# One probability tile in four transposed by a DMA instead of TensorE, and value projections in units of 512 pixels

## The reference

```python
def _L0_conv_ref(x, W_theta, b_theta, W_phi, b_phi, W_fuse, b_fuse):
    t, p, g = conv1x1(x, W_theta), conv1x1(x, W_phi), x          # 64, 64 and 128 channels
    f = softmax(einsum('ndq,ndk->nqk', t, p) / sqrt(64))
    return x + conv1x1(einsum('nqk,nck->ncq', f, g), W_fuse, b_fuse)

def _L1_conv_ref(x, gn_w, gn_b, q_w, ..., p_b):
    h_ = group_norm(x, gn_w, gn_b)                               # 32 groups
    q, k, v = conv1x1(h_, q_w, q_b), conv1x1(h_, k_w, k_b), conv1x1(h_, v_w, v_b)
    attn = softmax(einsum('bic,bcj->bij', q, k) * 128 ** -0.5)
    return x + conv1x1(einsum('bcj,bij->bci', v, attn), p_w, p_b)
```

## Time and profile before

| | before |
|---|---|
| time of three runs, median (lowest to highest) | 2015.87 us (2015.73 to 2016.52) |
| the profiled execution | 2016.01 us |
| its span | 2014.1 us |
| PE busy | 1975.8 us, 98% |
| DVE busy | 1727.1 us, 86% |
| ACT busy | 1546.7 us, 77% |
| POOL busy | 1356.0 us, 67% |
| mean granted TensorE clock | 0.994 |
| DMA | 68.01 MB |

### The profile page before, as it was taken

The page is one execution under the profiler, slowest core; times in us unless marked ns, Lnnn a source line. Parts: engine busy times, 40 slices in busy tenths (PEclk is TensorE's granted clock), DMA queues, the critical chain, the costliest instruction groups (busy, mean ns, idle before and its releaser), DMA issues.

```text
span 2014.1 us, 40574 instructions
## 1 busy us (share of the span) xinstructions
PE 1975.8 (98%) x11526; PEld 1334.6 (66%) x11526; DVE 1727.1 (86%) x2976; ACT 1546.7 (77%) x2696; POOL 1356.0 (67%) x1766
## 2 busy tenths in 40 slices
PE   6899999999999999999999999999999999999998
PEld 4666666666666666666666666666666666666664
DVE  6788888888888888888888888888888888888885
ACT  5677777777777777777777777777777778877775
POOL 4667666766667776667676677766676767777664
PEclk8999999999999999999999999999999999999999
DMA  1101111011111011110111110111101111101100
GB/s 53 48 27 37 36 34 37 23 36 42 36 31 36 26 36 36 42 31 21 41 37 36 31 36 26 36 36 42 31 23 40 36 36 31 36 26 37 33 6 22
DMA packets 29117, 68.01 MB, mean 34 GB/s; under 512 B 3616, under 2 KB 4512, under 8 KB 29088
## 3 DMA queue, kind: packets, MB, share of 16 engines
q1 hardware_dynamic: 29088, 67.65, 11.2%
HBM read 34.08 MB, written 16.78 MB: 25 GB/s over the span
## 4 chain that ended last, share of the span: by engine, by line
PE 76%; DVE 14%; issue 6%; ACT 3%; DVEq 0%; POOL 0%; DMA 0%; SPq 0%; ACTq 0%; POOLq 0%
PE o_ps L370 27%; PE s_ps L370 20%; PE t_ps L384 18%; DVE neg_raw L701 5%; PE m_ps L370 5%; PE m_ps L491 4%; DVE et L686 3%; ACT e L612 2%; DVE phi L769 1%; PE m_ps L493 1%; DVE x L720 1%; DVE theta L756 1%; DVE rden L677 1%; ACT et L548 0%; PE m_ps L475 0%
## 5 line engine op out<-in xcount | busy, mean ns | idle before, releaser
L863 POOL TENSOR_SCALAR e<-e,rden 128x1024 f32<-128x1024 f32 x512 | 575.8, 1125 | 482.3 <-DVE rden L677 479.2
L548 ACT ACTIVATE et<-t_ps 128x512 f16<-128x512 f32 x1024 | 560.3, 597 | 387.6 <-PE t_ps L384 387.2
L686 DVE TENSOR_TENSOR et<-t_ps,et 128x512 f16<-128x512 f32 x1024 | 659.7, 683 | 126.9 <-ACT et L548 120.7
L370 PE MATMUL o_ps<-et,v_hi 128*128 128x512 f16 x2048 | 696.3, 381 | 2.4 <-DVE y_sb L728 2.1
L384 PEld LDWEIGHTS t_ps<-ident_sb,e 128*128 128x128 f32 x4096 | 476.1, 141 | 118.7 <-DVE et L686 17.1
L384 PE MATMUL t_ps<-ident_sb,e 128*128 128x128 f32 x4096 | 540.4, 274 | 5.4 <-POOL e L863 2.6
L370 PE MATMUL o_ps<-et,v_lo 128*128 128x512 f16 x1024 | 388.0, 379 | 0.0
L370 PEld LDWEIGHTS o_ps<-et,v_hi 128*128 128x128 f16 x2048 | 204.5, 100 | 236.9 <-issue 50.3
L612 ACT ACTIVATE e<-s_ps,neg_max,exp_scale 128x1024 f32<-128x1024 f32 x256 | 309.8, 1210 | 4.4 <-DVE neg_max L704 2.4
L701 DVE TENSOR_REDUCE neg_raw<-s_ps 128x1 f32<-128x1024 f32 x256 | 309.5, 1209 | 1.4 <-PE s_ps L370 1.4
L698 DVE TENSOR_REDUCE neg_max<-s_ps 128x1 f32<-128x1024 f32 x256 | 310.6, 1213 | 0.0
(11 more groups left out here) (129 smaller groups left out, 2316.9 us busy)
## 6 DMA issues: line engine op xcount, KB each, us to landing
xs<-in_x SPq DMA_DIRECT2D x32, 512.0 KB, 3.7
phi<-phi SPq DMA_DIRECT2D x64, 256.0 KB, 3.1
xr<-in_x SPq DMA_DIRECT2D x32, 512.0 KB, 3.3
out_y<-y_sb SPq DMA_DIRECT2D x64, 256.0 KB, 2.1
w_f<-in_w_fuse_t SPq DMA_DIRECT2D x1, 64.0 KB, 2.7
ident_sb<-in_ident SPq DMA_DIRECT2D x1, 64.0 KB, 2.2
p_t<-in_p_w_t SPq DMA_DIRECT2D x1, 64.0 KB, 2.1
v_n<-in_v_w SPq DMA_DIRECT2D x1, 64.0 KB, 2.3
```

The costliest lines, as they stand in the source:

```text
L370: mm = pe.matmul(out, lhs_t, rhs, start=start and n == 0, stop=stop and n == len(terms) - 1)
L548: nc.scalar.activation(et[t // GROUP % 2][:, t % GROUP, GROUP * half:GROUP * (half + 1), :], t_ps[half][:, :].rearrange("k (b q) -> k b q" ...
L686: nc.vector.tensor_tensor(tile[:, KB + GROUP * half:KB + GROUP * (half + 1), :], t_ps[half][:, :].rearrange("k (b q) -> k b q", b=GROUP), ...
L863: return nc.gpsimd.tensor_scalar(*args)
```

## The change

**One tile in four is crossed.** Tiles 0, 4, 8 and 12 (`t % 4 == 0`) are no longer normalised by POOL, transposed by PE and copied out by ACT and DVE. Instead DVE makes `rden_e`, a scaled reciprocal (slot t + 2); ACT writes `e * rden_e` in float16 as the high half of `pair` (slot t + 2, between the exponential and `take_unit`); DVE writes what is left as its low half (slot t + 3, where `take_lo` stood); and SP issues one transposing DMA of the pair, 512 KB, straight into `et` (slot t + 3). The group's value product waits for it.

**Value units** cover 512 pixels: four blocks, each of three products of 128 columns (high with high weights, low with high, high with low) that add up in PSUM. The bank leaves through `stage` as the sum, POOL's addition goes, and high and low parts are split over 512 columns at once. There are four such units an image instead of eight, and slots 3, 12, 13 and 15 have no unit; `stage` has two buffers instead of four.

```diff
 NORM_MAX = 64.0
-UNITS = {0: "gn1", 1: "gn2", 2: "v2", 3: "v3", 4: "k0", 5: "k1", 6: "q0", 7: "w0", 8: "q1",
-         9: "tp0", 10: "w1", 11: "tp1", 12: "w2", 13: "w3", 14: "v0", 15: "v1"}
-STAGES = 4
-STAGE = {name: n % STAGES for n, name in enumerate(UNITS[s] for s in range(SLOTS) if UNITS[s][0] in "vw")}
+CROSSED = (0,)
+UNITS = {0: "gn1", 1: "gn2", 2: "v1", 4: "k0", 5: "k1", 6: "q0", 7: "w0", 8: "q1", 9: "tp0", 10: "w1", 11: "tp1",
+         14: "v0"}
+STAGES = 2
+STAGE = {"v1": 0, "w0": 1, "w1": 0, "v0": 1}
 H_SLOT = 2
...
                 return t[b] if isinstance(b, int) else t[bass.ds(b, 1)].rearrange("a c n -> c (a n)")
+            def transposes(i, s):
+                t = s - T_LAG
+                if not here(crossed_at, i, t):
+                    return
+                r = CROSSED.index(t % GROUP)
+                sp.wait_ge(s_pair, before(crossed_at, i, t) + 1)
+                sp.sem_inc(s_carrier)
+                sp.wait_ge(s_pv, or_none(before(group_at, i, t - t % GROUP) - 1))
+                sp.sem_inc(s_carrier)
+                sp.dma_start_transpose(et[t // GROUP % 2][:, t % GROUP, :, :],
+                                       pair[:, r, :, :].rearrange("q a n -> q (a n)")).then_inc(s_pair_t[r], 16)
             def image_loads(i, s):
...
                 if quarter == 0:
-                    pe.wait_ge(s_tlo, 2 * before(tile_at, i, first + GROUP))
+                    pe.wait_ge(s_tlo, 2 * before(turned_at, i, first + GROUP))
+                    for r in range(len(CROSSED)):
+                        pe.wait_ge(s_pair_t[r], 16 * before(group_at, i, first) + 16)
                     if s == PV_LAG:
...
                     if name[0] in "vw":
-                        for b in range(2):
-                            px = slice((2 * part + b) * P, (2 * part + b + 1) * P)
-                            pe.matmul(out[:, 2 * b * C:2 * (b + 1) * C], hi[:, px],
-                                      w[:, :, :].rearrange("p a c -> p (a c)"), start=True, stop=False)
-                            mm = pe.matmul(out[:, 2 * b * C:(2 * b + 1) * C], lo[:, px], w[:, 0, :],
-                                           start=False, stop=True)
+                        for b in range(GROUP):
+                            px = slice((GROUP * half + b) * P, (GROUP * half + b + 1) * P)
+                            mm = product(out[:, b * C:(b + 1) * C], [(hi[:, px], w[:, 0, :]), (lo[:, px], w[:, 0, :]),
+                                                                     (hi[:, px], w[:, 1, :])])
                     else:
...
                 t = s - T_LAG
-                if not here(tile_at, i, t):
-                    return
-                if half == 0 and t % GROUP == 0:
-                    act.wait_ge(s_pv, or_none(before(group_at, i, t) - 1))
-                act.wait_ge(s_tr, 2 * before(tile_at, i, t) + 1 + half)
+                if not here(turned_at, i, t):
+                    return
+                if half == 0:
+                    act.wait_ge(s_pv, or_none(before(group_at, i, t - t % GROUP) - 1))
+                act.wait_ge(s_tr, 2 * before(turned_at, i, t) + 1 + half)
                 nc.scalar.activation(et[t // GROUP % 2][:, t % GROUP, GROUP * half:GROUP * (half + 1), :],
                                      t_ps[half][:, :].rearrange("k (b q) -> k b q", b=GROUP),
                                      ACT.Copy).then_inc(s_thi, 1)
+            def pair_hi(i, s):
+                t = s - 2
+                if not here(crossed_at, i, t):
+                    return
+                r = CROSSED.index(t % GROUP)
+                act.wait_ge(s_rden_e, before(crossed_at, i, t) + 1)
+                act.wait_ge(s_pair_t[r], 16 * before(group_at, i, t - t % GROUP))
+                nc.scalar.activation(pair[:, r, 0, :], e[:, t % 4, :], ACT.Identity,
+                                     scale=rden_e[:, t % 4:t % 4 + 1]).then_inc(s_pair_hi, 1)
             def take_unit(i, s):
...
                 act.wait_ge(s_max, n + 1)
-                act.wait_ge(s_tr, or_none(2 * n - 6))
+                if s % GROUP in CROSSED:
+                    act.wait_ge(s_pair, before(crossed_at, i, s - GROUP + 1))
+                else:
+                    act.wait_ge(s_tr, 2 * before(turned_at, i, s - GROUP + 1))
                 scale = exp_scale[:, 0:1] if s % SLOTS >= PHASE else 1.0
...
                     exponentials(i, s)
+                    pair_hi(i, s)
                     take_unit(i, s)
...
                 nc.vector.reciprocal(rden[:, c:c + 1], den[:, c:c + 1]).then_inc(s_rden, 1)
+                if here(crossed_at, i, s - 2):
+                    dve.wait_ge(s_rden, before(tile_at, i, s - 2) + 1)
+                    nc.vector.tensor_scalar(rden_e[:, c:c + 1], rden[:, c:c + 1], E_SCALE, None,
+                                            ALU.mult).then_inc(s_rden_e, 1)
             def take_lo(i, s, half):
                 t = s - T_LAG
-                if not here(tile_at, i, t):
-                    return
-                dve.wait_ge(s_thi, 2 * before(tile_at, i, t) + 1 + half)
+                if half == 0 and here(crossed_at, i, t):
+                    r = CROSSED.index(t % GROUP)
+                    dve.wait_ge(s_pair_hi, before(crossed_at, i, t) + 1)
+                    nc.vector.scalar_tensor_tensor(out=pair[:, r, 1, :], in0=e[:, t % 4, :],
+                                                   scalar=rden_e[:, t % 4:t % 4 + 1], in1=pair[:, r, 0, :],
+                                                   op0=ALU.mult, op1=ALU.subtract).then_inc(s_pair, 1)
+                if not here(turned_at, i, t):
+                    return
+                dve.wait_ge(s_thi, 2 * before(turned_at, i, t) + 1 + half)
                 tile = et[t // GROUP % 2][:, t % GROUP, :, :]
...
             def normalise(i, s):
-                if not here(tile_at, i, s - 2):
+                if not here(turned_at, i, s - 2):
                     return
...
                 name = UNITS[(s - 1) % SLOTS]
-                n = before(values_at, i, s - 1)
-                total, part = (stage[:, STAGE[name], :, t, :] for t in range(2))
+                n, half = before(values_at, i, s - 1), int(name[-1])
+                src = stage[:, STAGE[name], :]
                 pool.wait_ge(s_evac, before(unit_at, i, s - 1) + 1)
-                nc.gpsimd.tensor_tensor(total, total, part, ALU.add).then_inc(s_sum, 1)
                 pool.wait_ge(s_pv, before(group_at, i, 0) if name[0] == "w"
                              else before(group_at, i, PHASE if s > PHASE else -PHASE))
                 values = (v_hi[1], v_lo[1]) if name[0] == "w" else (v_hi[0], v_lo[0])
-                hi, lo = (v[:, 2 * int(name[-1]):2 * int(name[-1]) + 2, :] for v in values)
-                pool.wait_ge(s_sum, n + 1)
-                rounded(hi, total, s_split_hi)
+                hi, lo = (v[:, GROUP * half:GROUP * (half + 1), :].rearrange("p b c -> p (b c)") for v in values)
+                rounded(hi, src, s_split_hi)
                 pool.wait_ge(s_split_hi, n + 1)
-                rest(lo, total, hi, s_split)
+                rest(lo, src, hi, s_split)
             def body(i):
```

More of the change, by code:

```diff
@@ L98, in group_at, with crossed_at, turned_at @@
         return int(g % GROUP == GROUP - 1 and tile_at(g))
+    def crossed_at(g):
+        return int(tile_at(g) and g % GROUP in CROSSED)
+    def turned_at(g):
+        return int(tile_at(g) and g % GROUP not in CROSSED)
     def unit_at(g):
@@ L103, in unit_at @@
         name = UNITS.get(s)
-        if name in ("tp0", "tp1", "v0", "v1"):
+        if name in ("tp0", "tp1", "v0"):
             return int(-1 <= i <= NB - 2)
-        if name in ("v2", "v3"):
+        if name == "v1":
             return int(0 <= i < NB)
@@ L113, in direct_at @@
     def direct_at(g):
-        return int(UNITS[g % SLOTS][0] in "tqk" and unit_at(g))
+        return int(UNITS.get(g % SLOTS, "-")[0] in "tqk" and unit_at(g))
     def values_at(g):
-        return int(UNITS[g % SLOTS][0] in "vw" and unit_at(g))
+        return int(UNITS.get(g % SLOTS, "-")[0] in "vw" and unit_at(g))
     def gn1_at(g):
@@ L217, in attention_pair @@
         h_hi, h_lo = sb("h_hi", [C, N], F32R), sb("h_lo", [C, N], F32R)
-        stage = sb("stage", [P, STAGES, 2, 2, C])
+        stage = sb("stage", [P, STAGES, HALF])
         theta2 = sb("theta2", [C, N], F32R)
@@ L226, in attention_pair @@
         et = [sb(f"et{n}", [P, GROUP, 2 * KB, P], F16) for n in range(2)]
+        pair = sb("pair", [P, len(CROSSED), 2, N], F16)
+        rden_e = sb("rden_e", [P, 4])
         neg_raw = sb("neg_raw", [P, 4])
@@ L251, in bank @@
         def bank(i, s):
-            return o_ps if first_units(i) and UNITS[s] in ("tp1", "v1") else m_ps
+            return o_ps if first_units(i) and UNITS[s] == "tp1" else m_ps
         s_wload0 = sem("layer0_weights_loaded")
@@ L277, in attention_pair @@
         s_tlo = sem("et_lo_ready")
+        s_rden_e = sem("rden_e_ready")
```

(18 more changed lines are left out.)

## The result

The changed kernel takes 2030.34 us (median of four runs, 2028.76 to 2030.38) against 2015.80 us of the kernel before in the same session: 1.007 of it, 95% interval 1.0052 to 1.0087. It is slower by 14.5 us, 0.45 us for each of 32 images. The forecast was 2009 and faster; the sign is wrong.

A forecast was written before the change was run, and what follows sets the result against it. PE, busy 98%, was taken to bound the kernel, with DVE next at 86%. Savings and added waits summed to -0.22 us per image, -7 us over 32 images: forecast 2009 us, range 1984 to 2040.

The forecast's parts named there:

- Transposes gone: On PE, four of sixteen tiles need no transposes, 0.88 us each: -3.52 us per image.
- Value units: On PE, four units priced at 1.32 us replace eight old ones at 0.83 per two: +1.96 us per image.
- The slot 12 wait: PE's wait for the VectorE phi at slot 12 goes, as no unit is there now: -0.34 us per image.
- Slot 1: PE reaches slot 1's transposes 1.0 us early and waits for VectorE's low parts: +0.78 us per image.
- The +6.48: For slot 1, the first half of t_ps came free 6.48 us after x's start at slot 15.
- Slot 7: pair_hi ahead of q_hi on ACT delays q_lo, so unit w0 starts late: +0.5 us per image.
- Slots 3 and 13: Said to have slot 7's pattern with small remainders: +0.1 us each per image.
- VectorE and GpSimd: Pair subtraction may meet GpSimd's value rest on the shared port at slots 11 and 15: +0.2 us per image.
- rival 2: Shared port holds the pair subtraction at slots 11 and 15: 2023 us, 2037 if GpSimd is held too; chance 0.25.
- The break-even I named: Shared-port holds decide the outcome from 0.42 us per image on.
- The transfer: SP's transposing DMA has about 10 us to land before the next pair_hi; costed at nothing.
- rival 3: Transfer lands later than 10 us, so ACT waits at pair_hi four times an image; 11 us gives above 2050; chance 0.1.

The follow-up runs named there:

- no cross: Changed kernel with the new value units only and no tile crossed (CROSSED empty): 2059.4 us, ratio 1.0218 to the kernel before.
- the small rest: Changed kernel with GpSimd making the values' low part for 16 of 512 columns in the loop's images: 2015.9 us, ratio 1.0003 to the kernel before.
- old units: Changed kernel keeping the crossing but restoring eight value units of 256 pixels and the GpSimd addition: 2047.0 us, ratio 1.0156 to the kernel before.
- the four moves: Changed kernel with pair_hi behind take_unit, x_max and x_bound at slot 8, v1 at slot 3, q_lo ahead of slot 7's maximum: 1954.4 us.

## Why the prediction was wrong

By its own steps, per image, from the slot table; "no cross" against "changed" isolates the crossing, "before" against "no cross" the units.

- *Transposes gone*, -3.52. Right: slots 11 and 15 are shorter by 0.88 and 0.87, and slots 3 and 7 would be but for their waits: -3.50.
- *Value units*, +1.96. Right: slots 2, 7, 10 and 14 grow by 0.87 to 0.89 and four slots lose a unit of 0.41: +1.88. A unit of twelve products runs from 1056.41 to 1057.70 in the changed kernel, 1.29 us; the price taken from the transposes, 0.11 for a load and 128 columns, was the right row.
- *The slot 12 wait*, -0.34. It was 0.46 (slot 12 is 0.87 shorter, 0.41 of which is the unit).
- *Slot 1*, +0.78. Measured +1.03, of which the small rest takes 0.21 back, so the chain without the port is 0.82: right in mechanism and size. (The +6.48 is one low part of 0.68 after 1042.31 and not half of 1.29, which would be +6.45; nothing hangs on it.)
- *Slot 7*, +0.5. Measured 0.64 (4.40 - 0.88 = 3.52 without a wait, 4.16 with): right in the main. With pair_hi moved 0.38 of it goes; 0.26 stays, where the rows gave 0.06 (q_lo's end at 1066.20 against 1066.14).
- **The first step that failed, "Slots 3 and 13 ... +0.1 each".** Measured 0.36 (3.12 - 0.88 = 2.24, 2.60 now) and 0.27 (3.46 to 3.73), of which 0.11 is the port's. At slot 3 the last value product starts at 1058.79, y_sb runs from 1059.40 to 1060.15, and the next group starts at 1060.30. Before, eight transposes, the scores and a unit lay between; now there are the scores alone. I counted what was taken from PE there and did not work out what it had covered; with v1 at slot 3 the unit covers it, and the wait is gone.
- **The second, "VectorE and GpSimd ... for the image I take 0.2".** Measured 0.53: slots 1 (0.21), 5 (0.21) and 13 (0.11). At slots 1 and 13 it is the pair subtraction's own length; at slot 5 it takes h_lo's hold and the split behind it together, and the hold's share alone is not shown. The mechanism, the two slots and the way through h_lo to slot 5 are those of rival 2; the size is about half of what that rival gave in full, yet more than twice what the forecast held. The break-even I named, 0.42 us of holds, was passed.
- At slot 10 a further 0.07 is lost; its cause is open.
- *The transfer*, nothing. Right: it lands 4.3 us after the issue, no ScalarE wait stands before pair_hi, and 3.8 us more before tile 8's cost nothing; rival 3 did not happen.

The sum with these sizes is -3.50 + 1.88 - 0.46 + 0.82 + 0.64 + 0.36 + 0.16 + 0.53 + 0.07 = +0.50, measured +0.44. Of the 0.7 between this and the forecast, 0.3 is the port and 0.3 slots 3 and 13. Rival 2 carried the right sign, and its range, 2023 to 2037, holds the result, but partly by luck: with its 0.53 in place of 0.2 the forecast's sum is +0.11, 2019 us, and slots 3 and 13 bring the rest.

The Trainium skill ("SBUF — State Buffer", SBUF: two separate sides) says that the second operation on the shared pair is blocked for the whole of the first. The trace agrees in direction and nearly in size: h_lo began 1.03 us before the pair's end and lost 0.87, the pair began 0.40 before v_lo's end and lost 0.20. In both some 0.2 us of the overlap was not lost, and so it was where the overlap was 0.55 (0.35 lost, old units) and 0.19 (none, pair_hi moved).

One thing was not foreseen in any rival: that the two parts of the change depend on each other. The crossing with the old units costs 31 us, and much of that is at slot 12 (1.27 us more than before) and at slots 5 and 6 (0.96), for which the sum has no such term.

## What to carry to other kernels

Work taken from a full engine is gained only down to the next chain at that place: for each slot that gets shorter, list which semaphore PE would meet there and when it is released, also where the trace shows no wait now. When an operation that read PSUM becomes one with two SBUF inputs, look for GpSimd operations in flight at that moment and price the meetings in both directions, with what queues behind each. And a change that loses may be a few moves short: the four moves here added no work and brought it from 1.007 to 0.970.

## What the hardware showed that was not expected

Issuing a transposing DMA of 512 KB occupied SyncE's queue for 1.79 and 2.95 us in the rows above (median of the changed kernel 1.88), where the plain loads and stores took 0.34 to 0.36 us in the same stretch, and the plain copy of the same 512 KB, in its own kernel, took 0.48 (last row):

```profile
1043.58 0.35 SPq L357 DMA_DIRECT2D xr<-in_x  x1
1045.89 1.95 SPq L351 DMA_TRANSPOSE et<-pair  x1
1058.76 0.36 SPq L368 DMA_DIRECT2D out_y<-y_sb  x1
...
1046.89 0.48 SPq L351 DMA_DIRECT2D et<-pair  x1
```

With x_max moved to slot 8, x_bound (128x1, two SBUF inputs) took 0.44 us in 28 of 32 images instead of 0.16, and ended with the GpSimd subtraction that it met, 1061.05 to 1061.49 against 1060.21 to 1061.48:

```profile
1061.05 0.44 DVE L836 TENSOR_TENSOR x_bound<-x_max,w_max 128x1 f32<-128x1 f32 x1
...
1060.21 1.27 POOL L942 TENSOR_TENSOR x_lo<-xs,x_hi 128x512 fp32r<-128x512 f32 x1
```

So even one column is held to the end of the other operation, as in the earlier trace rows. At its old place in the changed kernel it met none (0.16 in all 32 images); the move gave it a partner.
